# Two graph-attention layers and a third in one kernel: rows of targets turned behind the blocks of values, x turned a slot sooner

## The reference, cut to what matters

```
def gat_layer(x, mask, W, a_src, a_dst, bias, concat):
    xl = (x @ W).reshape(B, N, H, F)
    asrc = einsum('bnhf,hf->bnh', xl, a_src)
    adst = einsum('bnhf,hf->bnh', xl, a_dst)
    e = leaky_relu(asrc[:, :, None, :] + adst[:, None, :, :], 0.2)
    attn = softmax(where(mask[..., None], e, NEG_INF), axis=1)
    out = einsum('bsdh,bshf->bdhf', attn, xl)
    ...
h = elu(gat_layer(x, mask, W1, ...))             # 4 heads of 128
h = gat_layer(h, mask, W2, ...)                  # 1 head of 256
x = layernorm(x + h)                             # mask = adj > 0 or the diagonal
Wh = x @ W
e = leaky_relu(s_i[:, :, None] + s_j[:, None, :])
attention = softmax(where(adj > 0, e, -9e15), axis=1)
h_prime = leaky_relu(attention @ Wh)             # third layer, 1 head of 256
x = layernorm(x + h_prime)
```

## Time and profile before

| | |
|---|---|
| median of 3 runs | 906.83 us (906.67 to 908.46) |
| the profiled execution's own time | 906.18 us |
| its span (first to last instruction) | 904.3 us |
| instructions | 16988 |
| PE busy | 842.7 us, 93% |
| DVE busy | 742.3 us, 82% |
| ACT busy | 694.7 us, 77% |
| POOL busy | 266.7 us, 29% |
| chain that ended last, by engine | PE 65%, DVE 24%, issue 5%, ACT 4% |

### The profile page before, as it was taken

One profiled execution on the slowest core, in us unless ns is written; L12 is line 12 of the kernel. 1 busy time (PEld: TensorE's weight loads), 2 busy tenths in 40 slices (PEclk: granted clock), 3 DMA queues, 4 the chain that ended last, 5 costly groups with the idle time before them and its releaser, 6 DMA issues.

```text
span 904.3 us, 16988 instructions
## 1 busy us (share of the span) xinstructions
PE 842.7 (93%) x5996; PEld 789.3 (87%) x5996; DVE 742.3 (82%) x1922; ACT 694.7 (77%) x1302; POOL 266.7 (29%) x244
## 2 busy tenths in 40 slices
PE   6787979999999999999999999999999999999896
PEld 5687879898989989898998989899898989989675
DVE  6776798979797897979789796988979797897866
ACT  2666859789696978969687896969779696978553
POOL 0002010134332513433242243325124332434312
PEclk9898999999999999999999999999999999999999
DMA  9123131321223141122414112131311211100002
GB/s 250 47 71 71 47 94 49 94 48 48 73 69 94 48 117 48 47 75 68 94 48 117 48 42 79 69 95 48 117 48 47 71 71 25 47 24 1 24 1 70
DMA packets 100379, 59.81 MB, mean 66 GB/s; under 512 B 66244, under 2 KB 84804, under 8 KB 100296
## 3 DMA queue, kind: packets, MB, share of 16 engines
q1 hardware_dynamic: 100296, 58.73, 23.8%
HBM read 41.82 MB, written 8.50 MB: 56 GB/s over the span
## 4 chain that ended last, share of the span: by engine, by line
PE 65%; DVE 24%; issue 5%; ACT 4%; another core or an unknown queue 0%; DMA 0%; POOL 0%; SPq 0%; POOLq 0%; DVEq 0%; ACTq 0%
PE bUU L558 16%; PE bUU L580 11%; PE bG L652 10%; DVE junk L1008 8%; PE bG L670 7%; PE bG L640 5%; PE bUU L569 5%; PE bB L518 4%; DVE att L1008 4%; DVE y L1033 2%; DVE att L1055 2%; DVE y_lo L1045 2%; PE bG L631 1%; PE bUU L548 1%; PE bG L667 1%
## 5 line engine op out<-in xcount | busy, mean ns | idle before, releaser
L558 PE MATMUL bUU<-val,att 128*128 128x129 f32 x2048 | 249.3, 275 | 0.6 <-DVE att L1059 0.6
L558 PEld LDWEIGHTS bUU<-val,att 128*128 128x128 f32 x2048 | 241.2, 192 | 2.9 <-issue 1.0
L1059 DVE SCALAR_TENSOR_TENSOR att<-mask_n,att 128x2048 f32<-128x2048 bf16 x64 | 150.0, 2344 | 76.0 <-ACT att L802 73.5
L787 ACT ACTIVATE att<-bB,val 128x512 f32<-128x512 f32 x320 | 202.9, 707 | 5.2 <-PE bB L518 5.2
L802 ACT ACTIVATE att<-att 128x2048 f32<-128x2048 f32 x64 | 123.8, 1935 | 0.6
L426 POOL TENSOR_SCALAR var_eps<-moments 128x4 f32<-128x4 f32 x29 | 29.9, 1032 | 317.8 <-DVE moments L1101 317.8
L1008 DVE CUSTOM_DVE_ANT_0 junk<-mask_t,a_rows,val 128x512 bf16<-128x512 bf16 x168 | 116.7, 751 | 0.0
L569 PE MATMUL bUU<-val,att 128*128 128x257 f32 x480 | 110.0, 381 | 3.7 <-DVE att L1055 2.7
L860 ACT COPY val<-bG 128x524 f32<-128x524 f32 x62 | 37.3, 602 | 95.2 <-PE bG L670 95.1
L580 PE MATMUL bUU<-val3s,att 128*128 128x256 f32 x480 | 108.3, 379 | 0.2 <-DVE res L1089 0.2
L1008 DVE CUSTOM_DVE_ANT_0 junk<-mask_t,bA,val 128x512 bf16<-128x512 bf16 x152 | 104.1, 741 | 4.1 <-PE bA L518 4.1
(11 more groups left out here) (128 smaller groups left out, 1698.4 us busy)
## 6 DMA issues: line engine op xcount, KB each, us to landing
adj_in<-in_adj_dram SPq DMA_DIRECT2D x16, 1024.0 KB, 5.8
a_rows<-a_rows_dram SPq DMA_DIRECT2D x56, 256.0 KB, 3.8
x_in<-in_x_dram SPq DMA_DIRECT2D x16, 512.0 KB, 6.7
out_dram<-act SPq DMA_DIRECT2D x14, 512.0 KB, 2.9
mask_t<-mask_n SPq DMA_TRANSPOSE x64, 2.5
a_rows_dram<-val SPq DMA_DIRECT2D x56, 2.0 KB
att<-in_L_gnn_W_dram SPq DMA_DIRECT2D x4, 128.0 KB, 3.2
val<-in_L_gnn_W_dram SPq DMA_DIRECT2D x1, 512.0 KB, 7.2
```

Source lines behind the costliest of these rows:

```text
L558: ins = nc.tensor.matmul(to[:, (d % 2) * FX:(d % 2 + 1) * FX], p[:, s, d * P:(d + 1) * P], val1[u.batch % 2][:, s, u.index // 2, values], ...
L787: nc.scalar.activation(p[:, b], bB[:], ACT.Prelu, bias=a_col(u, b), alpha=SLOPE)\
L1059: nc.vector.scalar_tensor_tensor(flat(p), mask_n[u.batch % 3][:, 0:NB * N], BIG, flat(p), ALU.add, ALU.min)\
```

## The change

On PE, the block of values goes ahead of the turned head and the row of targets at pos 0 and 1, and ahead of the row of targets at pos 4. turn_x goes from the start of pos 5 to pos 4, behind attend (1) and ahead of sources_row. On ACT, x_out goes ahead of normalize at pos 5, and at pos 4 the copy of values_3's first block goes ahead of the second half of leaky, while that of its second block stays. On DVE, x_low goes from behind L3's tops and shifted_targets to ahead of them. Nothing is added or removed: every instruction of before is still there.

```
@@ PE
-                if pos == 5 and n + 2 < B:
-                    turn_x(n + 2)
                 if before:
                     attend(before, 0)
+                if pos in (0, 1) and batch:
+                    values_1(n + 1, pos + 1)
                 if oldest:
                     turn_head(oldest)
+                if pos == 4 and third:
+                    values_3(n - 2, (2, 3))
                 if after and after.row:
                     targets_row(after)
-                if pos in (0, 1) and batch:
-                    values_1(n + 1, pos + 1)
                 if pos == 2 and second:
...
                 if pos == 3 and third:
                     turn_x1(n - 2)
-                if pos == 4 and third:
-                    values_3(n - 2, (2, 3))
                 if before:
                     attend(before, 1)
+                if pos == 4 and n + 2 < B:
+                    turn_x(n + 2)
                 if later and not later.by_dma and g < LAST:
                     sources_row(later)
@@ ACT
                 if third_layer:
                     third_out(third_layer, 0)
+                if pos == 5 and n + 2 < B:
+                    x_out(n + 2)
                 if older:
                     normalize(older)
-                if pos == 5 and n + 2 < B:
-                    x_out(n + 2)
                 if pos == 0 and batch:
                     values_1_out(n + 1, 0)
+                if pos == 4 and third:
+                    values_3_out(n - 2, (0,))
                 if this:
                     leaky(this, (2, 3))
...
                 if pos == 4 and third:
-                    values_3_out(n - 2, (0, 1))
+                    values_3_out(n - 2, (1,))
@@ DVE
                 if last_head:
                     low_part(last_head)
+                if pos == 5 and n + 2 < B:
+                    x_low(n + 2)
                 if after:
                     tops(after)
                     shifted_targets(after)
...
-                if pos == 5 and n + 2 < B:
-                    x_low(n + 2)
```

## The result

The changed kernel takes 884.21 us (median of 4 runs, 882.46 to 885.78) against 907.64 us before (4 runs): a ratio of 0.974, 95% interval 0.9716 to 0.9765. The forecast was 882.7 us in a range from 878.5 to 892.0, at a chance of 0.92 for faster. The profiled execution took 883.62 us over a span of 881.7 us; before it was 906.18 us over 904.3 us.

What follows compares the result with a forecast made beforehand. PE, 93% busy, was bound apart from waits on one DVE chain. Twelve periods gain 18.1 us and n = 1 and 2 gain 6.0, together 24.1 off 906.18, plus 0.65 for the median: 882.7 us, range 878.5 to 892.

Steps and rivals of the forecast that it cites:

- The stalls that can be won: Twelve full periods: 15 PE waits for b_t, 10.4 us, 12 for x_lo, 5.8 us, plus 0.16 each: 20.5 us.
- step 5: Pos 5, x_out and x_low earlier: x_lo stall gone, DVE waits 0.35 us, 0.2 us a period lost at attend L2.
- steps 1 and 3: Blocks ahead of rows hide a 0.91 us stall at pos 0 and waits up to 0.9 us at pos 4.
- step 2: Pos 1, values_1 ahead of row of h1: no gain or cost in a full period; ACT gets it 0.9 us sooner.
- step 4: turn_x in pos 4 changes places with sources_row of L3; its need of values_3's last copy is hidden by 1.7 us.
- The rival that ends slower: ACT's last values_3 copy too late for turn_x, stopping PE once a period; 912.8 us at 4.2 us late; chance 0.05.
- step 6: n = 1 and 2: DVE's low_part waits go, b_t comes sooner; together 6.0 us, from 3.5 to 6.8.
- The clock rival: PE's clock falls at the gathered pause at n = 2, costing 2.5 us: 885.2 us; chance 0.20.
- The DVE rival: DVE takes over, attend L2 (0) waits 0.9 us in the periods: 891.1 us; chance 0.12.

Runs made afterwards that it cites:

- both edits: Changed kernel with the row of h2 behind values_2 and the first half of keep_edges of L2 ahead of L3's shifted_targets: 877.1 us, ratio 0.9672.
- the rows alone: Changed kernel without its three edits on x (turn_x, x_out, x_low as before), rows of targets behind the blocks: 888.14 us, ratio 0.9798.
- x alone: Kernel before with only the three edits on turn_x, x_out and x_low; rows and blocks as before: 904.98 us, ratio 0.9983.
- The row of h2: Changed kernel with, at pos 2 too, the row of targets of h2 behind its block of values_2: 877.37 us, ratio 0.9675.
- the later runs: The same file as the changed kernel, run again on a third chip: 881.68 us, ratio 0.9721 to the kernel before.

## Why the prediction was right, and where it was off

**The stalls that can be won** (20.5 us in twelve periods). Right in kind, about 1 us small. A stall for b_t costs its idle time + 0.16, as forecast (534.26 - 532.91 = 1.35 us from turn_head to the row of h0 before, 313.06 - 312.62 = 0.44 now, with 0.75 idle before):

```profile
532.91 0.60 PE L548 MATMUL bUU<-ident,y 128*128 128x128 f32 x4
```

A stall for x_lo costs its idle time + 0.24: the half of attend h3 ahead of it takes 305.35 - 303.64 = 1.71 us when values_1 follows at once, not the 1.79 that was read where something else followed, and the 2.28 of the earlier trace rows less 1.71 is 0.57 for 0.33 idle. That makes 10.4 + 5.8 + 15 x 0.16 + 12 x 0.24 = 21.5 us. With both edits the common period is 50.94 us, 1.72 below the average of before, 631.9 / 12 = 52.66. That the forecast's 20.5 / 12 = 1.71 is the same is partly luck, since 50.94 still holds a small wait, described under step 5.

**Pos 0 and pos 4** (steps 1 and 3). Right. With the rows behind the blocks alone the waits for b_t vanish in the twelve periods, and no wait of ACT for bB came up, not with the row of h2 later too.

**Pos 1** (step 2). It costs nothing in a full period: PE has no wait there, and ACT's wait for the block is 2.77 us (322.32) where it was 3.54 (546.16), sooner as forecast.

**turn_x in pos 4** (step 4). Right: no wait of L621 for a copy. The rival that ends slower has nothing in the trace for it.

**x_out and x_low** (step 5). The mechanism was right: the stall for x_lo is gone, and what is late next is keep_edges of L2 at attend L2 (0). The sizes were off. DVE's wait for x_hi is 0.18 us and not 0.35, and the forecast added a slow elu to it (0.3 in the first half of the run). They don't add up:

```profile
198.02 1.04 PE L621 MATMUL bG<-ident,x_in 128*128 128x128 f32 x8
198.89 0.87 DVE L1035 SCALAR_TENSOR_TENSOR y<-e,x 128x512 f32<-128x512 f32 x1
199.76 1.22 DVE L1071 TENSOR_TENSOR x_lo<-bG,x_hi 128x1024 fp32r<-128x1024 f32 x1
```

x_low starts 1.74 us behind turn_x here, with a slow elu and no wait, and as late (301.85 - 300.11) with a quick elu and the wait of 0.18; both periods take 51.05 us.

What PE loses at attend L2 (0) is more than the 0.2 us of the forecast. Its 3.47 us for this half was read where turn_head followed; with a block of values behind it the half takes 314.50 - 311.22 = 3.28 us if nothing holds it, as in the kernel with the rows alone:

```profile
311.22 3.63 PE L569 MATMUL bUU<-val,att 128*128 128x257 f32 x16
314.50 0.47 PE L667 MATMUL bG<-bias,ones_r 128*128 128x262 f32 x1
```

In the changed kernel it takes 310.73 - 307.14 = 3.59 us in the period shown and 3.55 in most, 0.27 too much, in two waits that PE's row is too coarse to show. One is for keep_edges: the first weights of attend L2 are loaded at 307.13, just behind the end of its first half (about 305.85 + 1.21 = 307.06). With that half moved ahead the attend half takes 3.45 us and the common period is 0.11 shorter, so this wait costs 0.11. The other 0.16 stays even then. Halfway through, the weight loads wait for the bank of h3's result, as the trace of another period shows:

```profile
206.94 0.19 PEld L569 LDWEIGHTS bUU<-val,att 128*128 128x128 f32 x1 [0.34 <-ACT x L814]
```

That is normalize of h3, which waits on DVE's invert behind both halves of keep_edges: the same DVE chain, by another door. So the twelve periods lost 12 x 0.27 = 3.2 us to it, not 2.4. They lost 2.8 more because four periods were longer (52.09, 51.94, 51.53 and 51.35 us). In all four, ACT stood still ahead of the same copy, that of values_2's last block in the middle of pos 3, though the block's last matmul had ended 1.0 to 1.9 us before:

```profile
442.06 0.37 ACT L855 COPY val<-bG 128x258 f32<-128x258 f32 x1 [1.94 <-remote]
...
545.07 0.38 ACT L855 COPY val<-bG 128x258 f32<-128x258 f32 x1 [1.80 <-remote]
...
647.37 0.37 ACT L855 COPY val<-bG 128x258 f32<-128x258 f32 x1 [1.12 <-PE bG L652]
...
698.96 0.37 ACT L855 COPY val<-bG 128x258 f32<-128x258 f32 x1 [1.18 <-PE bG L652]
```

The kernel before has such stops at the same copy too, 1.71 us at 456.84, 1.26 at 562.24 and four of 0.3 to 0.5; its larger waits at pos 4 (0.91, 0.47 and 0.17 us) come behind three of them. The row of L2 now absorbs them, but the order at pos 5 has no slack left for what is over: PE waits 0.6 us for keep_edges at 461.32. The forecast had seen the wait at pos 4 that such a stop makes, and not that it would come again further on. Every kernel's trace has some of these stops at this copy, of other lengths in each; what makes ACT stop was not tried and stays open.

The sum of this is 21.5 - 3.2 - 2.8 = 15.5 us where 16.5 were measured; the last 1.0, 0.1 us a period, is not placed. The forecast's 18.1 came as near as it did because its gain and its loss were both too small.

**n = 1 and 2** (step 6). 6.0 us forecast, 6.0 in the profile, and the pauses where they were said to be: 2.14 us before the row of h1, the row of h2 at 79.08, 4.0 us sooner than 83.07 (4.2 forecast), a pause of over 3 us at n = 2. At n = 1 the clock fell all the same, to a mean of 0.52 from 73 to 76.5 us, for some 3.5 us where it was 6.7 before (0.50 from 72.7 to 79.4); the forecast's hope for full clock there was wrong and its 4.2, cut from 4.5 for this, about right.

**The clock rival** (0.20). It is real, of the size forecast in two traces (2.65 and 2.6 against 2.5 us) and 1.5 us in a third, and it is not a question of which of two cases the kernel falls in: of six profiles with the same pause of 3.14 us at n = 2, two of them of the changed kernel itself, three show the half clock around or behind it and three do not. The Trainium skill's rule that recent activity decides ("TensorE: Matmul & The Clock Gate", What's actually happening) fits those three; the other three show that a pause of this length need not do it.

**The DVE rival** (0.12) names the right bound. Its size was reached only when x_out was put back: 8.3 us of waits and 892.8 us, against its 891.1.

**The experiments' own forecasts.** x alone was missed by 6.5 us, by the 0.35 that was 0.18, by taking all of before's periods for the quick ones, and by leaving out the waits at pos 4. The row of h2 was missed by 3 to 4 us, but most of that is the 884 it was counted from: against the 881.68 of the later runs it brought 4.3 us where 3 were forecast. Where they lie was missed: 1.1 us at n = 2, not 2.9, and 2.2 us behind the twelve periods, where I had not looked.

## What to carry to other kernels

When one slower chain of another engine serves several waits of PE, they are one stall in instalments: removing the first alone hands its time to the next (x alone, 0.2% gained), and putting a block of work that depends on nothing recent ahead of the waiting instruction removes the last. List, for each wait, what stands behind it in the queue and is ready already; that block is the cover, and here it also absorbed, at that place, stops that no order foresaw. Edits on three engines that feed each other should be tried whole: of the x edits, two without x_out were slower than none of them, and two without x_low no better. When a change gives less than 0.5%, compare traces part by part and not medians alone: the profile of one and the same file gave 2.6 us more or less with PE's clock and 1.8 us with ACT's stops.

## What was not expected of the hardware

- elu on DVE (two f32 inputs in SBUF) took 0.86 to 0.88 us where it started some 0.2 us behind an instruction of POOL's group at L435 (258.64 behind 258.43, 198.89 behind 198.68) and 0.68 us where it started ahead of one or up to 0.05 us behind (310.55 before 310.74 in the kernel with x alone, 300.99 before 301.52 in the changed one, 522.72 behind 522.67 before the change). In the order of before this is worth 0.2 us in the chain; in the changed kernel the wait for x_hi takes it up.
- PE's clock around the same pause of 3.14 us is full in three profiles and half in three others, for some 7 us in two of them (2.65 us a time) and for 3.5 us in the third (1.5 us).
- ACT stops for up to 2 us ahead of one and the same copy (values_2's last block at pos 3), in some periods of every trace. Two profiles of the changed kernel differ in it by 1.8 us in twelve periods.
